# Cross-attention and mixture-of-experts kernel: the Gelu table load, the bounds of the scatters, the loading of x and the instruction orders changed

## The reference, cut to what matters

```python
# L0_xattn: softmax(q k^T) over the context, applied to the normalized x
query = einsum('bnc,dc->bnd', ctx, Wq) + bq
key = einsum('bnc,dc->bnd', ctx, Wk) + bk
attention = softmax(einsum('bnd,bmd->bnm', query, key))
x = x + einsum('bln,bmn->blm', layernorm(x), attention)
# L0_ffn: top-1 of 8 experts, at most 160 tokens each
tokens = layernorm(x).reshape(1024, 256)
logits = tokens @ gate_weight.T
mask = one_hot(argmax(logits), 8); ranks = cumsum(mask) - 1; mask *= ranks < 160
out = probability * (gelu(tokens_of_e @ wi[e]) @ wo[e])      # wi: 256x1024, wo: 1024x256
x = x + out
```

## Time and profile before

| | us |
|---|---|
| runs of the kernel before | 114.33, 114.22, 113.61 (median 114.22) |
| profiled execution, its own time | 112.16 |
| span of its instructions | 110.4 |
| TensorE busy in the span | 102.0 |
| VectorE, ScalarE, GpSimd busy | 34.0, 31.2, 30.1 |

### The profile page before, as it was taken

One profiled execution on the slowest core, in us unless ns is written; L12 is line 12 of the kernel. 1 busy time (PEld: TensorE's weight loads), 2 busy tenths in 40 slices (PEclk: granted clock), 3 DMA queues, 4 the chain that ended last, 5 costly groups with the idle time before them and its releaser, 6 DMA issues.

```text
span 110.4 us, 1872 instructions
## 1 busy us (share of the span) xinstructions
PE 102.0 (92%) x694; PEld 88.6 (80%) x694; DVE 34.0 (31%) x148; ACT 31.2 (28%) x81; POOL 30.1 (27%) x54
## 2 busy tenths in 40 slices
PE   5999999999979999999999999999999999999800
PEld 5685887777769989998998998569999999886400
DVE  0019999999910144500510400220020010012010
ACT  3239584329672302341041041002203104100000
POOL 6401588385873000000420120213003003021330
PEclk9999999999999999999999999999999999999997
DMA  2899999999963599999999999940001001001100
GB/s 69 247 361 328 351 331 424 422 413 414 427 266 108 132 260 368 344 319 422 419 420 417 427 416 424 424 170 13 0 0 41 6 0 48 0 0 46 48 3 5
DMA packets 7969, 25.75 MB, mean 233 GB/s; under 512 B 916, under 2 KB 4760, under 8 KB 5912
## 3 DMA queue, kind: packets, MB, share of 16 engines
q1 hardware_dynamic: 6664, 23.24, 56.5%
q0 software_dynamic: 864, 2.12, 5.2%
q10 hardware_dynamic: 432, 0.27, 1.0%
HBM read 21.14 MB, written 4.76 MB: 235 GB/s over the span
## 4 chain that ended last, share of the span: by engine, by line
PE 75%; issue 7%; POOL 6%; DVE 5%; ACT 3%; POOLq 0%; ACTq 0%; DVEq 0%
PE ps L742 70%; POOL slots_dram L301 4%; PE ps L746 2%; PE ps L739 2%; POOL rows L292 1%; ACT ez L377 1%; DVE rows L496 1%; ACT L414 1%; POOL out L332 1%; PE ps L785 1%; DVE nmax L473 1%; DVE stats L560 0%; DVE y L719 0%; DVE turner L490 0%; ACT shared L385 0%
## 5 line engine op out<-in xcount | busy, mean ns | idle before, releaser
L742 PE MATMUL ps<-shared,wi_sb 128*128 128x160 f32 x256 | 36.3, 299 | 0.7 <-ACT shared L418 0.7
L742 PE MATMUL ps<-wo_sb,shared 128*128 128x256 f32 (+1 forms) x256 | 36.1, 380 | 0.0
L742 PEld LDWEIGHTS ps<-shared,wi_sb 128*128 128x128 f32 x256 | 35.1, 190 | 1.0 <-issue 0.8
L742 PEld LDWEIGHTS ps<-wo_sb,shared 128*128 128x128 f32 (+1 forms) x256 | 27.8, 150 | 6.0 <-issue 0.7
L332 POOL DMA_INDIRECT out<-y,got x10 | 9.8, 976 | 62.9 <-DVE y L719 43.4
L428 ACT ACTIVATE shared<-ps 128x480 f32<-128x480 f32 (+1 forms) x24 | 12.6, 526 | 49.4 <-PE ps L742 49.4
L719 DVE SCALAR_TENSOR_TENSOR y<-ps,share,got 128x256 f32<-128x256 f32 x10 | 4.8, 483 | 51.6 <-PE ps L742 31.0
L301 POOL DMA_INDIRECT slots_dram<-rows,slot x8 | 8.2, 1023 | 4.6 <-DVE slot L546 1.8
L742 PE MATMUL ps<-attended,shared 128*128 128x272 f32 x32 | 8.4, 402 | 0.2 <-ACT attended L345 0.2
L742 PEld LDWEIGHTS ps<-attended,shared 128*128 128x128 f32 x32 | 5.7, 189 | 1.4 <-ACT attended L345 0.3
L832 PE MATMUL ps<-shared 128*128 128x160 f32 x32 | 5.6, 314 | 0.2 <-DVE shared L555 0.2
(11 more groups left out here) (78 smaller groups left out, 74.7 us busy)
## 6 DMA issues: line engine op xcount, KB each, us to landing
wi_sb<-in_wi SPq DMA_DIRECT2D x8, 1024.0 KB, 16.5
wo_sb<-in_wo SPq DMA_DIRECT2D x8, 1024.0 KB, 18.6
slots_dram<-fill SPq DMA_DIRECT2D x1, 1300.0 KB, 13.1
shared<-in_x SPq DMA_DIRECT2D x2, 512.0 KB, 6.7
shared<-in_xT SPq DMA_DIRECT2D x2, 512.0 KB, 7.7
out<-rows SPq DMA_DIRECT2D x4, 256.0 KB, 5.6
got<-slots_dram SPq DMA_DIRECT2D x1, 780.0 KB, 5.6
got<-slots_dram SPq DMA_DIRECT2D x4, 130.0 KB, 2.4
```

The costliest lines, as they stand in the source:

```text
L742: return nc.tensor.matmul(dst, lhsT, rhs, start=(k == 0), stop=last)
```

## The change

- ScalarE: `preload_act_table(ACT.Gelu)` stands behind the copy of the gathered tokens, not ahead of it. The orders of k(1)/q(1), k(2)/q(2), `token` and `expz` are altered.
- GpSimd: two registers are set once with the two bounds, and the scatters are given them. A ninth scatter, all of whose indices are out of bounds, stands among the constants; the first real one waits for its completion. `first_rstd(1)`, `shifted_input`, `second_rstd` and `scatter` are in another order.
- x is loaded by ScalarE's queue, in three parts (tiles 0 and 1, 2 and 3, 4 to 7) with 2 KB runs in DRAM; SP no longer loads it. `bn1(n)` waits for its part.
- VectorE and TensorE have other orders in attention and routing; the work is the same.

```diff
-                sp.dma_start(x_sb[:, 4 * i:4 * i + 4, :], x_in_v[i]).then_inc(x_here[i], 16)
...
-            inputs(0)
             context(2)
             turned_inputs(0)
-            inputs(1)
...
+            last_slot = nc.gpsimd.alloc_register("last_slot")
+            nc.gpsimd.reg_mov(last_slot, E * CAP - 1)
...
+            pool.wait_ge(fill_done, 2)
+            nc.gpsimd.indirect_dma_start(
+                slots_dram, bass.IndirectOffsetOnAxis(ap=fill[:, INDEX:INDEX + 1].bitcast(I32), axis=0), fill[:], None,
+                bounds_check=last_slot, oob_is_err=False).then_inc(primed, 16)
...
+                    pool.wait_ge(primed, 16)
                     pool.wait_ge(filled, 16)
...
-                    bounds_check=E * CAP - 1, oob_is_err=False).then_inc(scattered, 16)
+                    bounds_check=last_slot, oob_is_err=False).then_inc(scattered, 16)
...
             second_rstd(0)
-            shifted_input(7)
             scatter(0)
+            second_rstd(1)
             scatter(1)
-            second_rstd(1)
-            second_rstd(2)
             scatter(2)
             scatter(3)
+            second_rstd(2)
             second_rstd(3)
...
+            for i, (a, z) in enumerate(X_PARTS):
+                act.dma_start(x_sb[:, a:z, :].rearrange("p (g t) h -> p g t h", t=2),
+                              x_in_v[a // 2:z // 2].rearrange("g p t h -> p g t h")).then_inc(x_here[i], 16)
             nc.scalar.preload_act_table(ACT.Exp)
...
-            nc.scalar.preload_act_table(ACT.Gelu)
...
             nc.scalar.activation(dispT[:, 1, 0, :], p_disp[1], ACT.Copy, scale=-1.0).then_inc(disp_sb, 1)
+            nc.scalar.preload_act_table(ACT.Gelu)
```

More of the change, by code:

```diff
@@ L42 @@
 W_FIRST = C + 2
+X_PARTS = [(0, 2), (2, 4), (4, 8)]
+X_PART_OF = [0, 0, 1, 1, 2, 2, 2, 2]
 W_ROW = 2 * C + 2 + HC * E
@@ L144, in xattn_moe @@
         ctx_here = [sem(f"ctx_here{i}") for i in range(NC_)]
-        x_here = [sem(f"x_here{i}") for i in range(2)]
+        x_here = [sem(f"x_here{i}") for i in range(len(X_PARTS))]
         xT_here = [sem(f"xT_here{i}") for i in range(2)]
@@ L389, in _ @@
             k(0)
+            k(1)
             q(1)
-            k(1)
             exp(0)
+            k(2)
             q(2)
-            k(2)
             exp(1)
@@ L400, in _ @@
             at(2)
+            token(0)
             expz(0)
-            token(0)
+            token(1)
             at(3)
             expz(1)
-            token(1)
             token(2)
             token(3)
+            token(4)
             expz(2)
-            token(4)
             token(5)
+            expz(3)
             token(6)
-            expz(3)
             token(7)
-            nc.scalar.preload_act_table(ACT.Gelu)
             act.wait_ge(disp_done, 2)
             nc.scalar.activation(dispT[:, 1, 0, :], p_disp[1], ACT.Copy, scale=-1.0).then_inc(disp_sb, 1)
+            nc.scalar.preload_act_table(ACT.Gelu)
             for e in range(E):
@@ L576, in _ @@
             bn1(2)
+            bn1(3)
+            st1(0)
+            mx(0)
+            mx(1)
             gate()
-            bn1(3)
             recip(0)
+            veps1(0)
             turn_by(0)
-            st1(0)
-            mx(1)
-            veps1(0)
             bn1(4)
@@ L586, in _ @@
             bn1(6)
+            shift(0)
             bn1(7)
+            st1(1)
+            mx(2)
             recip(1)
-            shift(0)
-            mx(2)
+            veps1(1)
             turn_by(1)
-            st1(1)
-            veps1(1)
-            x1(0)
             mx(3)
             recip(2)
-            bn2(0)
             shift(1)
             turn_by(2)
+            x1(0)
+            bn2(0)
+            scaled(0)
             x1(1)
-            scaled(0)
             summed(0)
@@ L606, in _ @@
             less(0)
+            value(0)
             veps2(0)
-            value(0)
+            first(0)
             recip(3)
-            x1(2)
-            first(0)
-            bn2(2)
             chosen(0)
             turn_by(3)
+            x1(2)
+            ranks(0)
+            bn2(2)
+            place(0)
             scaled(1)
-            ranks(0)
+            x1(3)
             summed(1)
-            place(0)
+            bn2(3)
             largest(1)
-            x1(3)
+            st2(1)
+            pick(0)
             less(1)
-            bn2(3)
+            veps2(1)
             value(1)
-            st2(1)
             x1(4)
             first(1)
-            veps2(1)
+            pick(1)
             chosen(1)
-            x1(5)
             bn2(4)
             scaled(2)
-            bn2(5)
-            summed(2)
-            st2(2)
-            largest(2)
-            veps2(2)
-            ranks(1)
-            less(2)
-            pick(0)
-            pick(1)
-            place(1)
-            value(2)
+            x1(5)
+            ranks(1)
+            summed(2)
+            place(1)
+            largest(2)
+            bn2(5)
             pick(2)
             x1(6)
+            st2(2)
+            bn2(6)
+            scaled(3)
+            x1(7)
+            summed(3)
+            less(2)
+            veps2(2)
+            bn2(7)
+            value(2)
+            st2(3)
             first(2)
-            bn2(6)
-            x1(7)
-            scaled(3)
+            largest(3)
             chosen(2)
-            summed(3)
-            bn2(7)
-            largest(3)
-            st2(3)
             veps2(3)
@@ L841, in _ @@
             q(1)
+            k(1)
+            en(0)
             gate_mean()
-            en(0)
-            k(1)
-            q(2)
-            k(2)
-            en(1)
+            en(1)
+            k(2)
+            q(2)
             at(0)
@@ L853, in _ @@
             xm(1)
+            forerunners(0)
+            at(2)
             xm(2)
-            at(2)
-            forerunners(0)
+            rk(0)
             xm(3)
-            rk(0)
             xm(4)
+            at(3)
             xm(5)
-            at(3)
             forerunners(1)
```

18 lines of the change are left out of this document (9 added, 9 removed).

## The result

Nineteen executions of each kernel on the same chip gave a median of 112.05 us before (111.58 to 114.33) and 112.94 us after (112.08 to 115.61). The ratio is 1.0072, with an interval of 1.005 to 1.0093. The change makes the kernel 0.7% slower, about 0.8 us, where I had forecast a gain of 1.2 us. The median of 114.22 us that stood ahead of the prediction was high; in all later comparisons the kernel before had a median of 112.05 to 112.28.

The account below looks back on a forecast made before the run. TensorE bounds the kernel from 32.45 us on; ahead of that VectorE and TensorE are full together. Table load 0.63, x parts 0.45 and registers 0.12 sum to 1.2 us: 114.22 to 113.0, range 111.9 to 114.7.

Parts of the forecast that it names:

- The x parts and VectorE's order: Attention and routing: statistics of tiles 0 to 3 move into VectorE's early idle time; gain 0.45 us, bounds gain 1.77, loss 1.4.
- Rival 3: Start: xT and context are served ahead of x, delaying VectorE's first maximum; slower, 116.7 us if landing at 11.05; chance 0.12.
- Table load: Ahead of expert 0: ScalarE's copy of gathered tokens starts with VectorE's, the load runs behind it; gain 0.63 us, bounds 0 and 0.63.
- Registers: Tail, between y and the last scatter: the MOVE of the bound goes; gain 0.12 us, bounds 0.03 and 0.46.
- The cap and GpSimd's roots: TensorE's first transposes of scattered rows: 1.15 us covers expert 0's 1.08 us; later roots behind four scatters covered by 0.1 us.
- Ninth scatter: Among GpSimd's constants: the extra scatter is not on the path; 0 us, bounds of a gain and a loss of 0.1.
- ScalarE's first copy: Start: three DMA issues delay the first table load to end at 4.3 us; the copy at 4.80 is covered by 0.5.

## Why the prediction was wrong, step by step

- **The x parts and VectorE's order: the step that failed.** "I put the second part at 7.4": it landed at 8.26 in the profiled execution, and at 8.29 to 10.62 in the six other traces with three parts. "I put it at 11.3" for the third: 12.26, and 13.02 and 12.66 with the old orders. I had reasoned from the total, and the total was nearly right: the 768 KB that had landed by 8.05 landed by 8.26. Two things were wrong. No half microsecond was saved by the second queue. And within the 768 KB x had come first because it stood ahead of the context chunk on one queue; on its own queue it lost that place, the chunk landed at 7.60 and x behind it. The working from there on held: 3.7 us behind the landing I had `at(0)`, and it came at 11.86, 3.60 behind 8.26, with a stand of 1.69 us for 0.4, because TensorE was free at 10.17 already and not at 10.7. `scaled(0)` came 0.83 later than forecast. The last gathers, put 0.45 earlier, came 0.61 later; 0.86 of these 1.06 us are the landing. x in three parts alone is a loss of about 1.5 us, at the edge of the working's own lower bound of 1.4, and x back on SyncE's queue won 1.3%. That rests on experiments from both sides.
- **Rival 3** had the mechanism: x served behind others and VectorE's program behind x. It was given 0.12, and its point, 9.75, was not reached in the profiled execution; the measured loss is a third of what it said, since landings between 7.4 and 9.75 already cost. The Trainium skill ("DMA: Bandwidth & Descriptors", section "Issuing engines are not separate DMA queues") says that DMAs of several issuers "will ultimately run on the same 16 DMA engines and interleave". The traces agree: all of x and xT was in by 12.26 us with two queues and by 12.33 with one, and with xT held back the third part landed at 11.22 instead of 13.02.
- **Table load.** The mechanism held, the size was off: 0.42 us ahead of expert 0 for 0.63. The copy of ScalarE's half does not start "some 0.05 us later" than VectorE's but 0.26 later (32.17 and 31.91), and the first Gelu was covered: the load ended at 33.78, the Gelu began at 34.53. No drain is seen behind the load, so the row's 1.28 us was right. The Trainium skill ("ScalarE: Activation LUTs", section "What ACT_TABLE_LOAD costs") counts 2.66 us for a switch. By that the load would have ended near 35.2, an estimate; the trace does not agree.
- **Registers.** Mis-sized: 0.52 us measured, 0.12 taken, 0.46 my upper bound. The bound was wrong because I took 0.30 us, the distance of scatters in a row, as the scatter's preparation. With the bound in a register the wait for y sits on the scatter itself, and 0.27 us is left from y to its start; with a MOVE in front, the wait sat on the MOVE and 0.73 us came behind it.
- **The cap and GpSimd's roots: the second step that failed.** Rightly named, wrongly judged. The fourth scatter should have ended near 26.5 and the roots near 28.0; they ended at 27.80 and 29.20. `expz` of the third batch, which waits for the third root, started at 28.64 instead of 26.62, and the fifth scatter at 30.09 instead of 29.64. So the 0.9 us by which the last scatter would land earlier did not come: it started 0.46 later (34.00 for 33.54), the second normalized tile moved from 39.05 to 40.06, and 0.73 us were lost at the transposes, for which the sum had nothing. The second root's shift pulled the second `expz` and the third scatter forward by 0.83 and 0.92 us, not by 2.
- **Ninth scatter, 0:** right. **ScalarE's first copy:** covered, right (4.56). **Undoing GpSimd's order** cost 2.25 us in the fastest execution and 6.6 by the medians (119.54 for 112.94): wrongly timed as it was, the order is needed by VectorE's.

Put together, in the profiled pair: the gathers missed the forecast by 1.06 us, the table by 0.16, the transposes by 0.73, and the tail gave 0.40 more than taken. 1.06 + 0.16 + 0.73 - 0.40 = 1.55 us is, to rounding, the distance from the forecast gain of 1.2 to the 0.36 us lost.

The predicted 113.0 us lies beside the measured 112.94 by chance alone: the median that I started from was 2 us too high, and the change was 2 us worse than forecast. The ratio is what was wrong: 0.99 forecast, 1.007 measured.

Left open: what the registers gain beyond 0.52 us, if anything; whether the split of the first four tiles adds to what the second queue costs, since three parts on SyncE's queue and two halves on ScalarE's were not run; how much of the changed kernel's last 0.2 to 0.5% is the new orders'; and why a part lands 2 us later in one execution than in another.

## What to carry to other kernels

A transfer moved to another queue gets no bandwidth of its own: here it shared the engines with what used to stand behind it, and lost its place in front. So an operand that is needed first belongs ahead of the others on one queue, and never more of an in-order engine's program behind its landing than has to be. Look at the last instruction of the kernel and at what stands between its release and its start: a constant in a register was worth more here than all reordering. And compare ratios of many executions, not one trace with one other: two traces here differ by half a microsecond before the first edit bears on them.

## What the runs showed of the hardware that was not expected

- An indirect DMA started 0.27 us after its release where the wait for it sat on it (tail with registers), and 0.77 to 0.84 us where the wait sat on a MOVE or a wait instruction in front (0.79 in the tail before, 0.84 and 0.77 for the third scatter before and with registers). With the waits exchanged the third and the fifth scatter started after 0.39 and 0.25 us.
- The second 256 KB part of x landed at 8.26, 8.29, 8.77, 8.98, 9.00, 10.55 and 10.62 in the seven traces of kernels with x on a second queue. The two halves on one queue landed at 6.50 to 7.79 and at 10.46 to 11.81 in seven traces.
- TensorE's granted clock reached the 2.4 GHz level at 6.45 us in the trace of before, at 4.29 in that of after, and at 4.27 to 7.18 in others. Six matmuls from 3.57 on took 3.02 us before; after, four from 5.18 on took 1.10. In kernels with the old order the first maximum started at 7.94 and 8.26 where the level came at 6.45 and 7.18, and at 7.43 where it came at 5.50: single profiles differ by half a microsecond from this alone.
- The clock fell back to 1.2 GHz during a stand of 3.44 us (low from 12.84 to 19.67), behind the stand of 2.53 us at the transposes (from 46.37 to 49.78), and behind the stands of 1.60 and 0.41 us there (from 43.02 to 46.43). Eight matmuls that take 1.19 us elsewhere took 2.18 in the first of these. A stand of TensorE can thus cost twice: its own time, and the slower matmuls behind it.
